# A graph-network kernel on one core: order lists of its own for the last round, with the projections in front and the attention of the pairs closer together

## What is computed

```python
m = embs @ map_w.T + map_b                      # embs: relu(layernorm(x)) of the graph
n = sem / norm                                  # m in 8 heads of 64, each row normalised
cos = einsum('bhsd,bhtd->bhst', n, n)           # "cos" products
cos_adj = (cos > THRESHOLD)
q = m @ q_w.T + q_b ; k = m @ k_w.T + k_b       # "q", "k" projections
scores = einsum('bhsd,bhtd->bhst', q, k) / 8    # "score" products, then masked
p_attn = softmax(scores) * keep
adj = cos_adj * p_attn
sem_h = embs @ gcn_map_w.T + gcn_map_b          # folded with gcn_W into one weight, "vv"
out = relu((adj @ sem_h) @ gcn_W.T / (adj.sum(-1) + 1))
x = x + out
```

## Time and profile before

| | |
|---|---|
| Time, median of 3 runs | 3765.98 us (3765.34 to 3768.06) |
| Time of the profiled execution | 3767.53 us |
| Span of the profiled execution, first to last instruction | 3765.7 us |
| Mean granted TensorE clock | 0.994 |
| TensorE busy | 3665.0 us, 97% |
| VectorE busy | 2723.6 us, 72% |
| ScalarE, GpSimd busy | 1695.4 us (45%), 1357.2 us (36%) |

### The profile page before, as it was taken

The page is one execution under the profiler, slowest core; times in us unless marked ns, Lnnn a source line. Parts: engine busy times, 40 slices in busy tenths (PEclk is TensorE's granted clock), DMA queues, the critical chain, the costliest instruction groups (busy, mean ns, idle before and its releaser), DMA issues.

```text
span 3765.7 us, 101867 instructions
## 1 busy us (share of the span) xinstructions
PE 3665.0 (97%) x31020; PEld 3224.1 (86%) x31020; DVE 2723.6 (72%) x9432; ACT 1695.4 (45%) x5075; POOL 1357.2 (36%) x2069
## 2 busy tenths in 40 slices
PE   8999999999999999999999999999999999999997
PEld 5888888888888888888888888888888888888885
DVE  3777777777777777777777777777777777777765
ACT  2444444444444444444444444444444444444443
POOL 2333433433433333334334334334333333343331
PEclk9999999999999999999999999999999999999998
DMA  2223323233233233333232332322332333332323
GB/s 94 91 96 106 99 99 107 94 108 102 96 112 102 96 109 100 102 104 104 97 107 98 100 107 94 109 102 96 112 102 96 108 100 102 103 104 98 107 86 107
DMA packets 250601, 381.35 MB, mean 101 GB/s; under 512 B 41328, under 2 KB 173968, under 8 KB 250576
## 3 DMA queue, kind: packets, MB, share of 16 engines
q1 hardware_dynamic: 250304, 380.73, 30.4%
q0 software_dynamic: 272, 0.30, 0.0%
HBM read 179.61 MB, written 167.77 MB: 92 GB/s over the span
## 4 chain that ended last, share of the span: by engine, by line
PE 89%; DVE 5%; issue 4%; DMA 1%; DVEq 1%; POOL 0%; ACT 0%; SPq 0%; POOLq 0%; ACTq 0%
PE bank L949 35%; PE bank L957 19%; PE bank L973 14%; PE bank L981 8%; PE bank L942 7%; PE bank L1090 3%; DVE h L675 1%; DVE x_mid L824 1%; PE bank L1024 1%; PE bank L1102 1%; DVE rel L794 1%; PE bank L898 1%; PE bank L1096 1%; DVE mv L669 0%; DVE rec L785 0%
## 5 line engine op out<-in xcount | busy, mean ns | idle before, releaser
L605 ACT ACTIVATE att<-att,nmax 128x256 f32<-128x256 f32 x1024 | 508.1, 501 | 83.5 <-DVE nmax L760 83.5
L771 DVE SCALAR_TENSOR_TENSOR att<-bank,att 128x256 f32<-128x256 f32 x1024 | 404.9, 421 | 33.0 <-ACT att L605 18.3
L949 PE MATMUL bank<-gT,w_k 128*128 128x256 f32 x3072 | 417.2, 285 | 0.5 <-DVE k L841 0.5
L949 PE MATMUL bank<-gT,w_q 128*128 128x256 f32 x3072 | 414.6, 284 | 2.7 <-DVE w_k L698 1.4
L949 PEld LDWEIGHTS bank<-gT,w_map 128*128 128x128 f32 x3072 | 370.7, 188 | 34.3 <-issue 25.8
L949 PE MATMUL bank<-gT,w_map 128*128 128x256 f32 x3072 | 396.9, 285 | 1.1 <-DVE gT L801 1.1
L949 PE MATMUL bank<-hT,w_qkv 128*128 128x256 f32 x3072 | 392.6, 284 | 4.4 <-DVE hT L801 4.4
L949 PEld LDWEIGHTS bank<-gT,w_k 128*128 128x128 f32 x3072 | 386.7, 189 | 8.2 <-DVE k L841 0.7
L957 PE MATMUL bank<-w_v,gT 128*128 128x512 f32 x1536 | 385.2, 399 | 0.0
L949 PEld LDWEIGHTS bank<-hT,w_qkv 128*128 128x128 f32 x3072 | 373.2, 189 | 13.6 <-DVE w_o L689 4.8
L949 PEld LDWEIGHTS bank<-gT,w_q 128*128 128x128 f32 x3072 | 380.3, 189 | 3.7 <-DVE w_k L698 2.2
(11 more groups left out here) (136 smaller groups left out, 7042.9 us busy)
## 6 DMA issues: line engine op xcount, KB each, us to landing
scratch<-att SPq DMA_DIRECT2D x256, 512.0 KB, 2.6
uT<-scratch SPq DMA_DIRECT2D x1024, 128.0 KB, 3.0
x_in<-x SPq DMA_DIRECT2D x64, 512.0 KB, 3.7
x_res<-x_mid SPq DMA_DIRECT2D x64, 512.0 KB, 2.9
out<-x_res SPq DMA_DIRECT2D x64, 512.0 KB, 2.8
adj<-adj SPq DMA_DIRECT2D x64, 64.0 KB, 1.9
att<-gcn_map SPq DMA_DIRECT2D x1, 1024.0 KB, 10.9
att<-map_rows SPq DMA_DIRECT2D x1, 1024.0 KB, 6.4
```

Source lines behind the costliest of these rows:

```text
L605: s_.activation(e_sl, e_sl, ACT.Exp, bias=nmax1[:, p, c, e:e + 1], scale=-1.0, accum_out=esum1[:, p, c, e:e + 1]).then_inc(exp1_done, 1)
L771: v_.scalar_tensor_tensor(e_sl, in_blocks(gram_bank[e][:, c * N:c * N + N]), COS_THRESHOLD, e_sl, ALU.is_gt, ALU.mult, accum_out=usum1[:, ...
L949: last = t_.matmul(dst, w(ws, k)[:, t * 128:t * 128 + 128], rhs[:, rs, k, :], start=(k == 0 and i == 0), stop=(k == KT - 1 and i == 2))
```

## The change

The change adds five lists for the last round alone and lets `steps` return them where there is no `n`. `LAST_POOL` and `LAST_SYNC` hold the same steps in the same order as before; the lists of TensorE, ScalarE and VectorE are new. No instruction is added or dropped and no wait is changed: each step waits for the same results as before.

```diff
+    LAST_TENSOR = [
+        ("score", 0), ("k", 2), ("score", 1), ("cos", 0), ("q", 2), ("vv", 0), ("cos", 1), ("score", 2), ("vv", 1), ("cos", 2),
+        ("k", 3), ("q", 3), ("value", 0), ("score", 3), ("cos", 3), ("back", 0), ("value", 1), ("back", 1), ("value", 2),
...
+    LAST = ((TENSOR, LAST_TENSOR), (SCALAR, LAST_SCALAR), (VECTOR, LAST_VECTOR), (POOL, LAST_POOL), (SYNC, LAST_SYNC))
...
         def steps(order, a, n, more):
+            if n is None:
+                return next(last for usual, last in LAST if usual is order)
             return [s for s in order if (isinstance(s, tuple) and a is not None)
```

## The result

The changed kernel takes 3760.88 us in the median of 22 runs (3756.53 to 3763.23), the kernel before in the same rounds 3766.61 us (3765.34 to 3768.59, 22 runs). The ratio is 0.9985, with a 95% interval of 0.9978 to 0.9991: 5.7 us less, which lies within the 0.2% that the forecast called no change, and clear of zero. The forecast was 3761.3.

What follows compares the result with a forecast made beforehand. TensorE bounds the untouched loop; in the last 54.7 us the score rope set the end. It won 6.9 us, the `uT` rope ate 2.2: 3765.98 - 4.7 = 3761.3 us, range 3758.4 to 3764.8.

Steps and rivals of the forecast that it cites:

- no change: Whole time: anything within 0.2% (7.5 us) can't be told from no change; chance of landing within, 0.89.
- Where the end is set: End of last round: score rope last before, `uT` rope after; shift 3 at 3745.2 in place of 3749.93, 4.7 us earlier.
- the `uT` rope: Last round's single `uT`: shift p waits for `value` p-1, so each pair costs at least one shift and one `value`.
- Spill 0: Front of last round: spill 0 issued at 3721.5 in place of 3724.56, 3.1 us earlier.
- `value` 0, held by TensorE's order: TensorE, last round: `value` 0 starts 3729.9 in place of 3731.80, held by TensorE's order, not shift 0; gain 2.1 us.
- Shift 1, bound by spill 1: SP's queue: spill 1 issued 3727.9, landing after 3.5 us, so shift 1 goes out at 3731.5 against 3733.18.
- Shift 1's issues: SP's queue: shift 1's four issues keep 2.41 us, as SP's list is the same; 0.7 us less if 1.74.
- `value` 1 at the low clock: TensorE, last round: `value` 1 takes 1.97 us after 2.8 us idle; at full clock 1.08, 0.9 us less.
- a stall for code: Rival: a 3.0 us halt of VectorE or TensorE ahead of 3729.9 cuts the gain to 1.7, 3764.3 us; chance 0.12.
- The rest: Last round from shift 2: shift 2 at 3738.7, `value` 2 at 3743.1, shift 3 at 3745.2, nothing changed after.
- one chain: Score rope, `score` 3 through flip b3 to spill 3: flip b3 ends at 3739.2, 6.9 us earlier than before.

Runs made afterwards that it cites:

- The kernel with `score` 3 late: Changed kernel with `score` 3 and what follows it put back behind `value` 1 and `back` 1: 47.09 us from `score` 0 to output issue, time 3765.79 us.
- the block out of the way in both orders: Code fetched earlier: 24 tiny matmuls ahead of `q` 2 with the old order up to `cos` 2, 42.67 us; 24 semaphore increments in the changed kernel, 41.38 us.
- the old front part: Changed kernel with the order of before up to `cos` 2, `flip_b` 2 and `exp_b` 2: 45.77 us from `score` 0 to output issue, time 3763.7 us.
- the third profile of the changed kernel: Changed kernel profiled again in the last series, nothing altered: 42.65 us from `score` 0 to output issue; time in that series 3761.64 us.
- the kernel with a second `uT`: Changed kernel with `x_in` as `uT` for the last round's odd pairs, so shift p waits for `value` p-2: 41.52 us from `score` 0 to output issue.

## Why the prediction was right

Step by step; predicted times are shifted by the 0.36 us by which the round began earlier.

- *Where the end is set.* Predicted: before, `score` 3 and its spill; after, the `uT` rope, with spill 3 issued behind shift 2 and landed 0.9 us ahead of `value` 2's end. Measured so: shift 3 at `value` 2's end, but spill 3 landed only 0.3 us ahead of it. The `uT` rope was last by so little that with a free `uT`, or with `value` 2 at full clock, spill 3 decided. The kernel with `score` 3 late shows that this step carries the gain, 47.09 us against 42.
- *Spill 0.* Predicted 3721.14, measured 3721.26.
- *`value` 0, held by TensorE's order.* Predicted 3729.5, measured 3730.21, without a wait for DMA. The 0.7 us are the `factor` held by GpSimd, a term that the sum didn't have, though the kernel before had the like in a place where nothing hung on it.
- *Shift 1, bound by spill 1.* Predicted 3731.1, measured 3732.32: 0.8 by the issue of spill 1, which inherits `factor` 0's delay, and 3.95 us for the spill and its hand-over where I had 3.6.
- *Shift 1's issues.* I kept 2.41 us because SP's list is the same. Measured 1.73. The step was mis-sized by 0.7 us (0.5 us up to shift 1's landing, which came 4.63 us behind the first issue) for a wrong reason: the delay isn't tied to SP's list but to a block of TensorE's code, which now fell on spill 1. I had ranked a stall for code as a rival of its own, a halt of the engine that needs the code; it came in another shape, as a slow DMA of somebody else.
- *`value` 1 at the low clock.* I took 1.97 us and measured 1.08, with 2.68 us of idle time ahead of it where I had 2.8. Mis-sized by 0.9 us. The rule of the Trainium skill, "TensorE: Matmul & The Clock Gate", section on HAM oscillation, that I followed (short bursts between DMA waits run cold every time), held for `value` 2 and 3 in all profiles of the changed kernel and for `value` 1 in none of the three.
- *The rest.* Shift 2 predicted 3738.3, measured 3738.14; `value` 2 3742.7 and 3742.64; shift 3 3744.8 and 3744.72. The gain of the round was put at 4.7 us and measured at 5.0.

So the mechanism was right, and the closeness of the number owes something to luck: +1.2 us up to shift 1's issue, -0.5 in shift 1 and -0.9 in `value` 1 nearly cancel. What the prediction did not see is how little the front part is worth. It described spill 0 as 3.1 us earlier and `value` 0 as 2.1; but with the block out of the way in both orders, 1.3 us of that reach the end (42.67 against 41.38 us), and in the changed kernel as it stands the block on spill 1 takes half of these away or all. Most of spill 0's gain is lost because shift 1 waits for spill 1 in the changed kernel, and spill 1 is issued only 0.55 us later in the round in the old order.

## What to carry to other kernels

At the end of a kernel, draw the two or three chains that could end last and compute each to the end, with the queue's own order as one of them: here the prediction gave one chain 6.9 us, and the other let about 5 through. Undo each half of a change alone before crediting it: one half looked worth 3.4 us in a profile and was worth about 1.3, since undoing it had also moved a block of code onto a transfer. A tiny VectorE operation with two SBUF inputs has no place on the critical path beside a long GpSimd operation; two entries further on it was free.

## What was not expected of the hardware

- A block of TensorE's code (0.02 MB, about 1 to 1.5 us of one DMA engine) holds up a data transfer in flight: a 512 KB spill landed after 2.6 us alone, after 3.4 to 3.7 directly behind a shift, and up to 5.3 with a block, 1.9 to 2.2 us behind the block's end in eleven spills. Four issues of shifts took 2.28, 2.41 and 2.85 us in place of 1.73 where a block started within 0.2 us ahead to 1.1 us behind the first issue. Thus added instructions on one engine can cost time on another's transfer. The Trainium skill, "Runtime: NRT & Kernel Launch", section on instruction fetch, describes fetching in blocks and calls the cost of crossing a block mostly hidden; here the data transfer beside it paid, with about 1.6 us in spill 1 of the old front part (5.3 us against 3.7 with the block moved away).
- TensorE's clock after an idle wait isn't a matter of that wait's length alone: `value` 1 ran 1.08 us behind 3.02 us of idle time in the third profile of the changed kernel and 1.97 us behind 2.97 us in the kernel with a second `uT`. In the first the granted clock was 1.00 until 3737.2, just before `value` 1's end, and 0.50 from 3737.6; in the second it was 0.50 from 3736.7, before `value` 1's start at 3737.56. What sets that moment stays open. In this round the low clock took about 2 us of TensorE's work on the chain. Matmuls without a reader brought it back, and the length fell by 0.65 to 1.4 us.
- The start of the last round varied by 2.6 us between profiles (3709.76 to 3712.32) with the same loop ahead of it. The clock ahead of it sorts them: in the six profiles with `score` 0 at 3709.8 to 3710.6 the mean granted clock was 0.91 in 3 to 80 us and 0.91 in 3645 to 3665 us, and in the eight with 3711.3 to 3712.3 one of the two was lower, 0.89 or 0.83. So a change in the last round is to be read as a length from an event in that round.
